# Vision block with routed experts: sums kept in the output tensor, and target rows for unused places of expert tiles

## The chip, the cores and the metric

The kernel runs on one core of a Trainium2 chip. The metric is the device time of one execution in microseconds (us); the median of three runs is compared.

## The reference

64 images of 196 tokens (12544 rows) of width 192. Patches are projected to tokens `h`; an attention branch with 12 heads is added; then a branch of 8 experts, of which each token takes the two with the highest router scores. Only this last part matters here:

```
score = relu(x @ Wr1.T + br1) @ Wr2.T + br2        # x = layernorm(h)
mask  = top 2 of 8;   w = softmax(where(mask, score, -inf))
for e in range(8):
    out += w[..., e:e+1] * (relu(x @ W1[e].T + b1[e]) @ W2[e].T + b2[e])
h = h + out
```

The result is an array of 12544 x 192 float32, which the kernel writes as `out_rows`.

## The kernel before

**Two phases.** The attention phase works through 32 pairs of images. For each pair SP stores `h` into the DRAM tensor `sums` (L405), loads it again (L410) and stores the attention sum there (L415); normalised rows go to `split_rows`. It ends at about 1170 us. Then `expert_phase` (L1318) runs.

**The expert phase.** All engines run the same loop over iterations `it`, each of six steps c = 0 to 5. Iterations 0 to 48 route one group of 256 tokens each: PE transposes and scores it, VectorE finds the two experts and their weights (`route`, `gates`), counts the place of each token within its expert (`find_place`), and GpSimd sends each row twice into `slots`, one list of rows for each expert (`send`, L1936). From iteration 10 on (`COMPUTE`) an expert tile of 512 rows is computed in each iteration: tile i = it - 10, 56 tiles (`NT`). `hidden` (L1558) makes the middle layer in six pieces; ScalarE writes the high part `mh` (L1885), VectorE the low part `ml` (L1797), and two steps later `project` (L1578) adds the piece to `y_bank`. In step 1 of the next iteration both engines evict with the gate (`y_out`, L1827 and L1893), and the first `project` of the next tile waits for that. GpSimd then issues four indirect DMAs of 128 rows each that add `y_out` to rows of `sums` (L1951); tile i waits until all adds of tile i-1 have landed (`added`).

**Which tiles.** Tiles 0 to 41 (`FULL`) are taken from the longest waiting list while routing goes on (`select`). The other 14 (`REST`) are planned at once, in the six steps of iteration 50 (`plan_rest`, L1717 to L1792, an increment of `plan` for each of 31 operations). A tile of these may overlap an earlier tile of its expert, may reach past the end of a list shorter than 512, or may be free (no rows left). Rows that don't count are sent to one of 512 extra rows behind the tokens in `sums`: `dest` is the token where `valid`, else the number of an extra row (`instead`, from `dummy_no`).

**Order around the change.** SP loads tile i two iterations ahead (`load_tile`, L1474): weights `wst`, transposed rows `xT`, and `tail` (token numbers and gates); for i >= 42 it waits for the whole plan (L1479), and each `tail` waits for the adds of tile i-3. On VectorE the order within a step is written out: `ml` of the piece, then the step's own work (gates, eviction, `find_place`, `select`, `tile_gates`, `route`), then the plan's part. `tile_gates` of tile i waits before `dest` until the adds of tile i-2 have landed. At the end SP waits for all adds and copies `sums` to the output:

```
sp.wait_ge(added, 16 * TJ * NT)
sp.dma_start(out.rearrange("(a b) e -> a (b e)", b=16),
             total_rows[0:ROWS_ALL].rearrange("(a b) e -> a (b e)", b=16)).then_inc(copied, 16)
sp.wait_ge(copied, 16)
```

## Time and profile before

| | us |
|---|---|
| median of 3 runs | 2125.47 (2125.39 to 2127.91) |
| the profiled execution, its own time | 2127.24 |
| its span, first to last instruction | 2125.5 |
| busy: PE / VectorE / ScalarE / GpSimd | 1868.0 / 1442.9 / 1280.5 / 1138.5 |
| mean granted TensorE clock | 0.934 |
| moved by DMA | 382.72 MB, mean 180 GB/s |

Engines in the rows: PE is TensorE, DVE VectorE, ACT ScalarE, POOL GpSimd, SPq the queue of SyncE. Times are us from the start of the span unless marked ns. A row names the line of the kernel, the operation, output<-input by the program's names without buffer numbers, and how often (x). In brackets or behind a bar stands how long the engine sat idle before it, and what ended that; such releasers are inferred, and where several things were awaited, the last by the profile is named. Ends of matmuls are modelled, so starts are compared, not ends.

### The profile page before, as it was taken

What the parts mean: (1) busy time and instruction counts of PE and PEld (TensorE: products, weight loads), DVE (VectorE), ACT (ScalarE), POOL (GpSimd) and SP (SyncE); (2) the same over time, 40 slices, a digit from 0 to 9 for tenths busy, and PEclk for the clock granted to TensorE, in tenths of its full rate; (3) what the DMA queues carried; (4) which work ended last, traced back from release to release, by engine and by line L of the source; (5) the groups of instructions that cost most, each with busy time, mean ns of one, the idle gap of its engine ahead of it and who ended that gap; (6) DMA issues with size and microseconds to landing.
All of it is one profiled execution on the core that took longest, in us unless ns stands there. A gap on an engine that the chain in (4) does not pass through costs nothing. (4 is left out here: it accounts for less than half of the span.)

```text
span 2125.5 us, 54282 instructions
## 1 busy us (share of the span) xinstructions
PE 1868.0 (88%) x17949; PEld 1387.1 (65%) x17949; DVE 1442.9 (68%) x4460; ACT 1280.5 (60%) x2661; POOL 1138.5 (54%) x1069
## 2 busy tenths in 40 slices
PE   4978988998888999889895679999999999999990
PEld 3656766666666766666663457777777777767760
DVE  4768888888988889888884446555555655554430
ACT  4758888888888888888886234434444343433330
POOL 4335564645555465555532346666666666654442
PEclk8879999999999999999986569999999999999995
DMA  4575665665656565565642267888787878799877
GB/s 152 169 204 168 192 207 160 196 181 173 194 176 198 175 194 170 180 187 188 192 146 87 84 171 185 203 189 210 180 208 189 197 204 187 199 195 180 189 146 196
DMA packets 362727, 382.72 MB, mean 180 GB/s; under 512 B 144532, under 2 KB 326096, under 8 KB 358288
## 3 DMA queue, kind: packets, MB, share of 16 engines
q1 hardware_dynamic: 320912, 338.66, 55.1%
q0 software_dynamic: 41664, 42.12, 11.5%
q8 instruction: 86, 1.41, 0.3%
q14 instruction: 65, 0.53, 0.1%
HBM read 232.83 MB, written 135.46 MB: 173 GB/s over the span
## 5 line engine op out<-in xcount | busy, mean ns | idle before, releaser
L1885 ACT ACTIVATE mh<-mid_bank 128x512 bf16<-128x512 f32 x336 | 201.0, 598 | 467.8 <-PE mid_bank L1576 356.6
L1797 DVE SCALAR_TENSOR_TENSOR ml<-mid_bank,mh 128x512 bf16<-128x512 f32 x336 | 231.8, 690 | 347.6 <-ACT mh L1885 338.6
L859 DVE TENSOR_REDUCE row_max<-s_bank 98x2 f32<-98x392 f32 x768 | 394.7, 556 | 57.6 <-PE s_bank L635 55.4
L1056 ACT ACTIVATE probs<-t_bank 98x392 f32<-98x392 f32 x768 | 340.5, 500 | 110.7 <-PE t_bank L651 106.6
L1951 POOL DMA_INDIRECT sums<-y_out,tail x168 | 265.2, 1579 | 171.5 <-DVE y_out L1827 124.1
L1590 PE MATMUL y_bank<-wst,mh 128*128 128x192 bf16 x1344 | 330.0, 246 | 8.7 <-DVE y_out L1827 8.4
L1593 PE MATMUL y_bank<-wst,ml 128*128 128x192 bf16 x1344 | 330.1, 246 | 0.0
L1592 PE MATMUL y_bank<-wst,mh 128*128 128x192 bf16 x1344 | 329.8, 245 | 0.0
L635 PE MATMUL s_bank<-k_stack,q_stack 96*98 96x196 f16 x1536 | 235.7, 261 | 56.9 <-DVE row_max L859 43.2
L1232 POOL TENSOR_TENSOR x_lo<-x_buf,x_hi 128x588 f16<-128x588 f32 x128 | 170.7, 1346 | 178.6 <-DVE x_b L924 76.2
L651 PE MATMUL t_bank<-q_stack,k_stack 104*98 104x196 f16 x1536 | 227.5, 261 | 38.2 <-ACT probs L1056 34.8
L1936 POOL DMA_INDIRECT slots<-row_r,spot x196 | 191.2, 976 | 97.4 <-issue 56.7
L635 PEld LDWEIGHTS s_bank<-k_stack,q_stack 96*98 96x98 f16 x1536 | 145.9, 127 | 107.3 <-DVE row_max L859 93.2
L651 PEld LDWEIGHTS t_bank<-q_stack,k_stack 104*98 104x98 f16 x1536 | 153.3, 129 | 80.0 <-ACT probs L1056 75.1
L543 PE MATMUL p_bank<-wtok_h,x_hi 128*98 128x192 f16 x768 | 193.6, 252 | 10.3 <-POOL x_lo L1232 10.2
L545 PE MATMUL p_bank<-wtok_h,x_lo 128*98 128x192 f16 x768 | 192.9, 251 | 0.0
L544 PE MATMUL p_bank<-wtok_l,x_hi 128*98 128x192 f16 x768 | 192.8, 251 | 0.0
L664 PE MATMUL o_bank<-probs,v_buf 98*32 98x196 f32 x3072 | 175.7, 348 | 4.4 <-ACT probs L1056 2.6
L1590 PEld LDWEIGHTS y_bank<-wst,mh 128*128 128x128 bf16 x1344 | 134.3, 100 | 41.9 <-issue 21.3
L1080 ACT COPY q_stack<-m_bank 8x784 f16<-8x784 f16 x192 | 154.6, 805 | 6.1 <-PE m_bank L675 1.5
L1592 PEld LDWEIGHTS y_bank<-wst,mh 128*128 128x128 bf16 x1344 | 131.0, 97 | 19.6
L1951 POOL DMA_INDIRECT sums<-y_out,dest x56 | 86.9, 1552 | 96.1 <-DMA sums<-y_out,dest 44.9
(236 smaller groups left out, 4530.7 us busy)
## 6 DMA issues: line engine op xcount, KB each, us to landing
wst<-packed SPq DMA_DIRECT2D x56, 1584.0 KB
x_buf<-in_x_t SPq DMA_DIRECT2D x32, 1176.0 KB, 7.9
q_stack<-stack_parts SPq DMA_DIRECT2D x288, 98.0 KB, 2.5
k_stack<-stack_parts SPq DMA_DIRECT2D x288, 98.0 KB, 2.6
stack_parts<-qk_hi SPq DMA_DIRECT2D x32, 588.0 KB, 2.9
stack_parts<-qk_lo SPq DMA_DIRECT2D x32, 588.0 KB, 3.1
sums<-h_buf SPq DMA_DIRECT2D x32, 294.0 KB
h_in<-sums SPq DMA_DIRECT2D x32, 294.0 KB
```

Of the source, the lines that this page charges most:

```text
L543: nc.tensor.matmul(out, x_hi[:, f, tokens], wtok_h[:, f, :], start=(f == 0), stop=False)
L545: ins = nc.tensor.matmul(out, x_lo[:, f, tokens], wtok_h[:, f, :], start=False, stop=(f == PCH - 1))
L635: last = nc.tensor.matmul(s_bank[hh % 2][0:HALF, u, 0:TOKENS], q_stack[st.q][0:PARTS, head, head_cols(st, u)], k_stack[st.q][0:PARTS, head ...
L651: last = nc.tensor.matmul(out, k_stack[st.q][:, head, head_cols(st, v)], q_stack[st.q][:, head, head_cols(st)], start=True, stop=True)
L859: nc.vector.reduce_max(row_max[st.odd][:, :, hh:hh + 1], s_bank[hh % 2][0:HALF, :, 0:TOKENS], AX.X).then_inc(max_ready, 1)
L1056: nc.scalar.activation(probs[st.odd][:, hh], t_bank[hh % 2][0:HALF, :, 0:TOKENS], ACT.Exp).then_inc(probs_ready, 1)
L1590: nc.tensor.matmul(o, mh[n % MID][:, cols], high, start=(c == 0 and j % 2 == 0), stop=False, skip_group_check=True)
L1592: nc.tensor.matmul(o, mh[n % MID][:, cols], low, start=False, stop=False, skip_group_check=True)
L1593: last = nc.tensor.matmul(o, ml[n % MID][:, cols], high, start=False, stop=False, skip_group_check=True)
L1797: nc.vector.scalar_tensor_tensor(ml[n % MID][:], mid_bank[n % MID_PS][:], 0.0, mh[n % MID][:], ALU.max, ALU.subtract).then_inc(ml_ready, 1)
L1885: nc.scalar.activation(mh[n % MID][:], mid_bank[n % MID_PS][:], ACT.Relu).then_inc(mh_ready, 1)
L1951: nc.gpsimd.indirect_dma_start(out=total_rows, out_offset=bass.IndirectOffsetOnAxis(ap=to, axis=0), in_=y_out[q][:, j, :], in_offset=None, ...
```

## The change

`sums` goes: the attention phase's rows and all adds go to the output tensor, and the copy at the end is gone. As the output has no extra rows, each row of a tile needs a real token, and one that occurs once in its DMA. Rows that only overlap keep their own token (`keep` now from `below`), rows of a free tile take tokens 0 to 511, and rows past the end of a short list take a token that the expert lacks. Their gate is multiplied by `valid`, so they add zeros. The tokens that an expert lacks are found among the first 1024 (`number_others` in iterations 1 to 4 numbers them, `place_others` in iteration 20 splits the numbers, `mark_others` on VectorE and `list_others` on PE in iterations 50 and 51 turn them into a list by a matmul with one-hot matrices, and `plan_spare_rows` in iteration 51 picks from it). `load_tile` waits for step 25 of the plan instead of the last. Constants: `SPARE_TILES` = 8, `HOT` = 3 buffers, `LIST_AT` = 20, `PLAN` = 39, `TILES_KNOWN` = 25.

```diff
 COMPUTE = SELECT + 2
 REST = NT - FULL
 AHEAD = 4
+SPARE_GROUPS = 2 * T // GT
+SPARE_TILES = SPARE_GROUPS * GTILES
+HOT = 3
 GATE_BLOCKS = 3
 
...
                 if i < FULL:
                     sp.wait_ge(selected, PICK * (i + 1))
                 else:
-                    sp.wait_ge(plan, PLAN)
+                    sp.wait_ge(plan, TILES_KNOWN)
...
             sp.wait_ge(added, 16 * TJ * NT)
-            sp.dma_start(out.rearrange("(a b) e -> a (b e)", b=16),
-                         total_rows[0:ROWS_ALL].rearrange("(a b) e -> a (b e)", b=16)).then_inc(copied, 16)
-            sp.wait_ge(copied, 16)
...
+
+            def list_others(e):
+                if 0 <= e < EXPERTS:
+                    pe.wait_ge(placed, PLACE * FGROUPS)
+                    pe.wait_ge(hot_ready, e + 1)
+                    for b in range(SPARE_TILES):
+                        last = nc.tensor.matmul(spare_ps[:, e, :], hot[e % HOT][:, b, :], listed[:, b, e, :],
+                                                start=(b == 0), stop=(b == SPARE_TILES - 1))
+                    last.then_inc(spares_ready, 1)
...
+                    list_others(FCH * (it - FULL - SELECT) + c - LAG)
                     if 0 <= n - LAG < FCH * NT:
                         project(n - LAG)
...
+            def number_others(g):
+                if 0 <= g < SPARE_GROUPS:
+                    shape = [P, GTILES, EXPERTS]
+                    if g == 0:
+                        dve.wait_ge(masks_set, 4)
+                    else:
+                        dve.wait_ge(number_ready, 3 * g)
+                    dve.wait_ge(placed, PLACE * g + 1)
+                    nc.vector.tensor_tensor(rank[:], place[:], first_slot[:].unsqueeze(1).to_broadcast(shape),
...
+                    nc.vector.scalar_tensor_tensor(away[:], chosen[g % 2][:], 2.0 * ROWS_ALL, rank[:], ALU.mult,
...
+                    nc.vector.scalar_tensor_tensor(number[:, GTILES * g:GTILES * (g + 1), :], away[:], float(GT * g),
+                                                   row_no[:, 0:GTILES].unsqueeze(2).to_broadcast(shape), ALU.add, ALU.add
...
+            def place_others(part):
+                shape = [P, SPARE_TILES, EXPERTS, TJ]
+                if part == 0:
+                    dve.wait_ge(number_ready, 3 * SPARE_GROUPS)
+                    nc.vector.tensor_copy(number_i[:], number[:]).then_inc(listed_ready, 1)
+                    dve.wait_ge(listed_ready, 1)
+                    nc.vector.tensor_scalar(column_i[:], number_i[:], 7, None, ALU.arith_shift_right
+                                            ).then_inc(listed_ready, 1)
+                    dve.wait_ge(listed_ready, 2)
+                    nc.vector.tensor_copy(column[:], column_i[:]).then_inc(listed_ready, 1)
+                elif part == 1:
+                    dve.wait_ge(listed_ready, 3)
+                    nc.vector.scalar_tensor_tensor(lane[:], column[:], -float(P), number[:], ALU.mult, ALU.add
+                                                   ).then_inc(listed_ready, 1)
+                    nc.vector.tensor_tensor(in_column[:], column[:].unsqueeze(3).to_broadcast(shape),
+                                            tile_no[:, 0:TJ].unsqueeze(1).unsqueeze(1).to_broadcast(shape),
+                                            ALU.is_equal).then_inc(listed_ready, 1)
+                elif part == 2:
+                    dve.wait_ge(listed_ready, LISTED - 1)
+                    nc.vector.tensor_tensor(listed[:], in_column[:],
+                                            token_f[:].unsqueeze(2).unsqueeze(2).to_broadcast(shape), ALU.mult
+                                            ).then_inc(listed_ready, 1)
+
+            def mark_others(e):
+                if 0 <= e < EXPERTS:
+                    shape = [P, SPARE_TILES, P]
+                    dve.wait_ge(listed_ready, LISTED)
+                    wait(dve, spares_ready, e - HOT + 1)
+                    nc.vector.tensor_tensor(hot[e % HOT][:], lane_no[:].unsqueeze(1).to_broadcast(shape),
+                                            lane[:, :, e:e + 1].to_broadcast(shape), ALU.is_equal
+                                            ).then_inc(hot_ready, 1)
+
...
-                    step(nc.vector.tensor_tensor(valid[:], above[:], below[:], ALU.mult))
...
                 elif part == 5:
+                    step(nc.vector.tensor_tensor(valid[:], above[:], below[:], ALU.mult))
+                    step(nc.vector.tensor_scalar(keep[:], below[:], -1.0, None, ALU.mult))
+                    step(nc.vector.tensor_scalar(unused[:], below[:], -1.0, 1.0, ALU.mult, ALU.add))
+                    step(nc.vector.tensor_scalar(is_free[:], rest_f[:], float(EXPERTS), None, ALU.is_ge))
+                    dve.wait_ge(plan, 33)
+
+            def plan_spare_rows(part):
+                def step(ins):
+                    ins.then_inc(plan, 1)
+
+                if part == 2:
+                    dve.wait_ge(spares_ready, EXPERTS)
+                    step(nc.vector.tensor_copy(other_row[:], spare_ps))
+                    dve.wait_ge(plan, 34)
+                elif part == 3:
+                    shape = [P, REST, TJ, EXPERTS]
+                    step(nc.vector.tensor_tensor(past_other[:], is_expert[:].unsqueeze(2).to_broadcast(shape),
+                                                 other_row[:].rearrange("p e j -> p j e").unsqueeze(1)
+                                                 .to_broadcast(shape), ALU.mult))
+                    dve.wait_ge(plan, 35)
+                    step(nc.vector.reduce_sum(other_f[:].unsqueeze(3), past_other[:], AX.X))
+                elif part == 4:
                     shape = [P, REST, TJ]
-                    nc.vector.tensor_scalar(keep[:], valid[:], -1.0, None, ALU.mult)
-                    step(nc.vector.tensor_scalar(unused[:], valid[:], -1.0, 1.0, ALU.mult, ALU.add))
-                    dve.wait_ge(plan, 30)
-                    step(nc.vector.tensor_tensor(instead[:], unused[:], dummy_no[:].unsqueeze(1).to_broadcast(shape),
-                                                 ALU.mult))
+                    step(nc.vector.tensor_tensor(spread[:], row_no[:].unsqueeze(1).to_broadcast(shape),
+                                                 is_free[:].unsqueeze(2).to_broadcast(shape), ALU.mult))
+                    dve.wait_ge(plan, 37)
+                    step(nc.vector.tensor_tensor(harmless[:], spread[:], other_f[:], ALU.add))
+                    dve.wait_ge(plan, 38)
+                    step(nc.vector.tensor_tensor(instead[:], unused[:], harmless[:], ALU.mult))
...
@@ -1814,9 +1921,13 @@
                     wait(dve, added, 16 * TJ * (i - 1))
                     nc.vector.tensor_tensor(dest[q][:], kept[:], instead[:, i - FULL, :], ALU.bitwise_or
                                             ).then_inc(gate_step, 1)
+                    nc.vector.tensor_tensor(gate_sum[:], gate_m[:], words[:, :, 3], ALU.add).then_inc(gate_step, 1)
+                    dve.wait_ge(gate_step, base + 4)
+                    nc.vector.tensor_tensor(gate[q][:], gate_sum[:], valid[:, i - FULL, :], ALU.mult
+                                            ).then_inc(gate_step, 1)
                 else:
                     dve.wait_ge(gate_step, base + 1)
-                nc.vector.tensor_tensor(gate[q][:], gate_m[:], words[:, :, 3], ALU.add).then_inc(gate_step, 1)
+                    nc.vector.tensor_tensor(gate[q][:], gate_m[:], words[:, :, 3], ALU.add).then_inc(gate_step, 1)
...
                     elif c == 3:
+                        number_others(it - 1)
                         select(it - SELECT)
...
                         route(it)
                     if it == FULL + SELECT:
                         plan_rest(c)
+                    elif it == FULL + SELECT + 1:
+                        plan_spare_rows(c)
+                    elif it == LIST_AT:
+                        place_others(c)
+                    mark_others(FCH * (it - FULL - SELECT) + c)
...
-            nc.gpsimd.iota(dummy_no[:], [[P, TJ]], base=ROWS_ALL, channel_multiplier=1,
+            nc.gpsimd.iota(lane_no[:], [[1, P]], base=0, channel_multiplier=0,
                            allow_small_or_imprecise_dtypes=True).then_inc(masks_set, 1)
+            nc.gpsimd.iota(token_f[:].rearrange("p (g j) -> p g j", g=SPARE_GROUPS), [[GT, SPARE_GROUPS], [1, GTILES]],
+                           base=0, channel_multiplier=GTILES, allow_small_or_imprecise_dtypes=True
+                           ).then_inc(masks_set, 1)
...
-    sums = nc.dram_tensor("sums", (ROWS_ALL + T, DIM), F32).ap()
...
-                        stack_parts, by_pair(sums[0:ROWS_ALL]), by_pair(split), router)
-        expert_phase(nc, packed, slots, sums, split.rearrange("(g t) e -> g t e", t=GT), router, out)
+                        stack_parts, by_pair(out), by_pair(split), router)
+        expert_phase(nc, packed, slots, out, split.rearrange("(g t) e -> g t e", t=GT), router)
```

## Rows read from the trace of the kernel before

**Rows 1.** Windows: from:to and length, busy us per engine (xcount), PEclk, DMA share, GB/s.

```profile
2092.00:2126.00 34.00, 0.00 (x0) 0.00 (x0) 0.00 (x0) 0.00 (x0) 0.00 (x0) 0.50 0.89 283
```

**Rows 2.** DMA issues: xcount, KB each, median us to landing.

```profile
out_rows<-sums SPq DMA_DIRECT2D x1, 9408.0 KB, 32.8
```

**Rows 3.** Timeline of GpSimd and of SP: start us, length, instruction, idle before it.

```profile
2035.02 1.55 POOL L1951 DMA_INDIRECT sums<-y_out,dest  x1 [6.81 <-DVE gate L1819]
...
2040.59 1.55 POOL L1951 DMA_INDIRECT sums<-y_out,dest  x1 [0.30 <-issue]
2049.01 1.55 POOL L1951 DMA_INDIRECT sums<-y_out,dest  x1 [6.87 <-DVE gate L1819]
...
2088.73 1.55 POOL L1951 DMA_INDIRECT sums<-y_out,dest  x1 [0.30 <-issue]
...
2092.26 0.65 SPq L1507 DMA_DIRECT2D out_rows<-sums  x1
```

**Rows 4.** Chain that ended last, in order of time: start us, us, what.

```profile
2040.59 7.65 DMA sums<-y_out,dest
...
2079.03 3.35 DMA sums<-y_out,dest
```

**Rows 5.** Timeline of VectorE.

```profile
1873.07 0.74 DVE L1827 TENSOR_SCALAR y_out<-y_bank,gate 128x192 f32<-128x192 f32 x2 [1.41 <-DMA sums<-y_out,tail]
...
1885.85 0.74 DVE L1827 TENSOR_SCALAR y_out<-y_bank,gate 128x192 f32<-128x192 f32 x2
...
2048.33 0.16 DVE L1815 TENSOR_TENSOR dest<-kept,instead 128x4 int32<-128x4 int32 x1 [2.43 <-DMA sums<-y_out,dest]
```

**Rows 6.** Timeline of GpSimd, first adds of tiles 36 and 37.

```profile
1829.62 1.61 POOL L1951 DMA_INDIRECT sums<-y_out,tail  x1 [3.01 <-DVE y_out L1827]
...
1845.11 1.61 POOL L1951 DMA_INDIRECT sums<-y_out,tail  x1 [2.97 <-DVE y_out L1827]
```

**Rows 7.** Timeline of VectorE, early iteration, scores of a group.

```profile
1190.72 0.17 DVE L1636 TENSOR_TENSOR score<-small_bank,br_rows 128x16 f32<-128x16 f32 x1 [3.87 <-PE small_bank L1542]
```

**Rows 8.** Groups by line and shape, VectorE: busy us, mean ns | idle before.

```profile
L943 DVE TENSOR_TENSOR tilde<-beside,padded 128x1176 f32<-128x1176 f32 x32 | 43.8, 1368 | 0.0
...
L1742 DVE TENSOR_TENSOR past<-tile_no,scan 128x112 f32<-128x112 f32 x1 | 0.3, 266 | 0.0
```

**Rows 9.** The same groups in the stretch 1870 to 1885.8 alone.

```profile
L1797 DVE SCALAR_TENSOR_TENSOR ml<-mid_bank,mh 128x512 bf16<-128x512 f32 x7 | 4.8, 692 | 3.4 <-ACT mh L1885 2.5 <-DVE expert_i L1772 0.6 <-DVE done_f L1762 0.2
L1827 DVE TENSOR_SCALAR y_out<-y_bank,gate 128x192 f32<-128x192 f32 x2 | 0.7, 414 | 1.4 <-DMA sums<-y_out,tail 1.4
```

**Rows 10.** Timeline of PE, first projection of tile 41.

```profile
1886.73 0.24 PE L1590 MATMUL y_bank<-wst,mh 128*128 128x192 bf16 x1
```

**Rows 11.** Timeline of GpSimd, first adds of tiles 40 and 41.

```profile
1886.86 1.55 POOL L1951 DMA_INDIRECT sums<-y_out,tail  x1 [5.25 <-DVE y_out L1827]
...
1900.10 1.55 POOL L1951 DMA_INDIRECT sums<-y_out,tail  x1 [6.12 <-DVE y_out L1827]
```

**Rows 12.** Timeline of PE: matmuls of 8 and of 192 columns.

```profile
1841.00 0.17 PE L1551 MATMUL small_bank<-chosen,before 128*128 128x8 bf16 x1
...
1841.10 0.17 PE L1555 MATMUL small_bank<-chosen,ones 128*128 128x8 bf16 x1
...
2029.91 0.25 PE L1592 MATMUL y_bank<-wst,mh 128*128 128x192 bf16 x1
2029.99 0.25 PE L1593 MATMUL y_bank<-wst,ml 128*128 128x192 bf16 x1
```

**Rows 13.** Waits of SP, 1860 to 1900: waiter <- what, us, times, longest.

```profile
SPq L1480 <- DVE instead L1791: 4.6, 1, 4.6
```

**Rows 14.** Windows, columns as in rows 1.

```profile
1962.00:2062.00 100.00, 98.34 (x816) 70.04 (x813) 40.70 (x92) 36.97 (x69) 44.29 (x29) 1.00 0.91 182
```

**Rows 15.** Groups by line and shape, GpSimd from 1200 us on.

```profile
L1951 POOL DMA_INDIRECT sums<-y_out,tail x168 | 265.2, 1579 | 171.5 <-DVE y_out L1827 124.1 <-issue 38.4 <-DMA sums<-y_out,tail 9.0
...
L1951 POOL DMA_INDIRECT sums<-y_out,dest x56 | 86.9, 1552 | 96.1 <-DMA sums<-y_out,dest 44.9 <-DVE gate L1819 27.0 <-issue 16.2
```

46 lines of the change are left out of this document (38 added, 8 removed).

## The prediction

> **What bounds the kernel now.** I read the page's slices first, then the busy time by stretch, then the end of the timeline, and from there backwards along the chain of waits. The reader is to see three stretches.
>
> (a) The last 34 us belong to one transfer. After 2092 no engine is busy while the DMA engines work at 0.89 [rows 1]: that is the copy of L1507, issued at 2092.26 and landed 32.8 us later, at 2125.06 [rows 2, 3]. It starts 0.15 us after the last adding DMA lands: that was issued at 2088.73 [rows 3], and with 3.35 us to land, as the one of 2079.03 had [rows 4], it lands at 2092.1. Nothing overlaps the copy and only 0.4 us follow it.
>
> (b) In tiles 42 to 55 the expert phase runs to the adding DMAs, not to PE. GpSimd issues four per tile, and tile i waits until those of tile i-1 have landed. One link: first issue at 2035.02, last at 2040.59 (5.6 us), 7.65 us to land, 0.77 us until the next tile's first issue at 2049.01: 14.0 us [rows 3, 4]. (The gate named as releaser there is the next tile's; GpSimd does not wait for it.) VectorE even stands 2.43 us before `dest`, waiting for such a landing [rows 5]. A tile of PE work takes about 12.8 us there, which is the distance from one tile's eviction at 1873.07 to the next at 1885.85 [rows 5].
>
> (c) Before, up to tile 39, the distance from one tile's adds to the next is 15.5 us and they start when `y_out` is ready [rows 6]: PE and the router set the pace, and the chain of adds, 14.0 us as above, has some 1.5 us of slack.
>
> **The change part by part.**
>
> The copy goes. What is then last is the landing of the last adds at 2092.1 and the same 0.4 us behind it. Gain: 2125.06 - 2092.1 = 33.0 us, all on the path, since nothing lay beside it [rows 1 to 4]. The stores and loads of the attention phase, and all adds, now go to the output tensor instead of `sums`: same shapes, same queues, same counts. No row shows 768-byte adds to the output. The nearest row is the copy itself, which writes 9408 KB into it in 32.8 us, 294 GB/s [rows 2], so the output takes writes at a good rate; I put the difference at nothing, with 2 us either way over 56 tiles and 96 row transfers for other addresses.
>
> Numbering the tokens (`number_others`, 3 small VectorE operations in each of four early iterations). An operation of 16 elements starts about 0.2 us after its predecessor when it waits for it, so 0.6 us. VectorE stands idle 3.87 us in each of these iterations until the next scores come [rows 7]: hidden. Without that cover it would be 2.4 us. The GpSimd constants (one iota more, one larger) lie ahead of its wait for VectorE's memsets: hidden too.
>
> Listing (`place_others`, 6 operations at iteration 20, of 64 to 256 elements). By the size law below about 1.8 us over three steps. VectorE has 1 us and more of idle time in most steps, but `ml` and the eviction behind it are needed by PE: 0.2 us, between 0 and 1.8.
>
> Marking (`mark_others`, 8 operations on VectorE at iterations 50 and 51). This is the term that costs. Size: 128x1024 with two float32 inputs. The 128x1176 operation of L943 takes 1368 ns and the 128x112 one of L1742 266 ns [rows 8], so 1.036 ns an element, 1.21 us for 1024, and 1.13 us from start to start, as successors start 0.08 us before an end. Place: each is issued at the end of a step, behind `plan_rest`, and ahead of the next step's `ml`, so seven of them stand ahead of the eviction of tile 40. That stretch (1869.4 to 1885.85) has VectorE idle 3.4 us before `ml` and 1.4 us before `y_out` [rows 9]. Of these 4.8 us some 0.3 us before `y_out` and 0.2 us of waiting for its own result remain, so 4.3 us can be filled. Added: 7 x 1.13 + 0.1 (one more small plan operation) = 8.0 us. Overflow: 3.7 us. Who waits: PE, whose first projection of tile 41 came at 1886.73, directly after `y_out` of 1885.85 was written [rows 5, 10]. So PE, the eviction of tile 41 and the adds of tiles 40 and 41 move by 3.7 us. Both starts of adds were released by `y_out` [rows 11], and from 42 on each follows from the landing before it, so the shift stays to the end. What could take part of it back: the weights of tiles 43 and 44 were loaded beside these adds, and with the adds later the loads are ahead of them. Bounds 0.5 and 5.
>
> Counting on PE (`list_others`, 64 matmuls of 128x128 weights on 4 columns). Nearest rows: the five matmuls of 8 columns of `count` start 25 ns apart [rows 12], so 8 x 25 ns = 0.2 us for each expert, 1.6 us in all. Those of seven experts fall before the projection that waits for the eviction anyway, the eighth after it: 0.2 us. Upper bound: each of them priced as a 192-column matmul of L1592 and L1593, 80 ns apart [rows 12], 5.1 us in all, of which 0.6 us falls after that wait. The Trainium skill speaks against the short spacing ("TensorE: Matmul & The Clock Gate", section "Back-to-back issue gap"): in a stream where each matmul has its own weight load it gives about 81 ns for each at 128 columns and says that the isolated figure counts too little at small sizes. The trace disagrees for the small form; by the page the term would be 0.65 us instead of 0.2.
>
> The plan. SP loaded tile 42 only after the whole plan, waiting 4.6 us for `instead` [rows 13]; now it waits for step 25, which comes earlier by two parts but behind four marks: about 1.5 us sooner. PE never waited for that load: nothing. `plan_spare_rows` waits on VectorE for PE's eighth group; behind it stands one `ml`, and PE needs that two steps later: nothing (0 to 1 us). The two extra small operations of `tile_gates` in the last 14 tiles stand behind the wait for the adds; PE has 14.0 - 12.8 = 1.2 us of slack there against some 0.15 us: nothing.
>
> Rows that add zeros now hit real tokens instead of 512 rows behind them. Each add still moves the same 128 rows: nothing.
>
> Sum: -33.0 + 3.7 + 0.2 + 0.2 = -28.9 us. The profiled execution took 2127.24 us with a span of 2125.5, so it would take 2098.3, with a span of 2096.6. The median of the runs shown is 1.77 us lower, so I predict 2125.47 - 28.9 = 2096.6 us.
>
> **The rivals.**
>
> The shift is taken back (15%). For it: the DMA engines are at 0.91 in the tiles after 45 [rows 14], so the chain of adds partly waits for bandwidth, and loads that ran ahead leave it free. Against: loads are themselves released by landings. If 3 us of the 3.7 vanish: 2093.6.
>
> The marking costs more (14%). For it: four adds of tile 39 and of tile 40 are issued in just that stretch. Only the most general row bears on it: GpSimd's add instruction takes 1579 ns beside router work on VectorE and 1552 ns in the last tiles without it [rows 15], so VectorE disturbs it little. If each of 8 issues is held for half a mark, 0.6 us, 5 us come on top: 2101.6. The Trainium skill ("SBUF — State Buffer", on the shared port pair) says that a VectorE operation with two SBUF inputs and a GpSimd one exclude each other for a whole instruction; by its rule the issues would be blocked, and this is the case it argues for. The trace shows 27 ns.
>
> Adds into the output land later (4%, slower). Mechanism: adds read and write 768-byte rows of a tensor that so far only took one large copy. Place: the last leg of each tile's chain. Price: x us per landing costs 14x in tiles 42 to 55, and beyond the slack of 1.5 us also 42(x - 1.5) before them [rows 6]. It eats the gain of 28.9 us where 56x = 28.9 + 63, x = 1.64 us (a landing of 9.3 us for 7.65). At x = 2.1 us it costs 29.4 + 25.2 = 54.6 us: 2151. Against: nothing in the copy's row hints at a slow tensor.
>
> The copy's end was not the program's end (1%): if some fixed work of like length follows the last transfer, no change, 2125. Against: 0.4 us follow it in the trace.
>
> **How the numbers follow.** Forecast 63%, 2094.5 to 2098.8. Taken back 15% (2092.5 to 2094.5). Costs more 14% (2098.8 to 2105). Other addresses gain more than 33 us 3%. Slower 4%, none 1%. The range 2091 to 2102 leaves out the last three, 8%, and the upper half of the costlier case, 7%; the few per cent that remain are for the small terms put at nothing. A difference of 0.2% (4.3 us) is what a measurement of this kernel can tell from none. Faster: 63 + 15 + 14 + 3 = 95%; same 1%; slower 4%.
>
> **What would show it.** No transfer after the last add, and the span's end within 1 us of that landing. At 1870 to 1890 eight 128x1024 operations of about 1.2 us on VectorE, the eviction of tile 40 about 3.7 us later against that of tile 39, and PE idle before the first projection of tile 41. Starts of adds 42 to 52 still 13 to 14 us apart. Iterations 1 to 4 and 20 as long as before. The prediction is wrong if the landing of the adds has changed, if the 15.5 us pace of tiles up to 39 has changed, or if the marks are hidden.

## The result and the profile after

| kernel | median of the device time | range, runs |
|---|---|---|
| before | 2125.49 us | 2125.39 to 2127.91, 4 |
| after | 2102.77 us | 2097.00 to 2105.89, 4 |

Ratio 0.9888, interval 0.9871 to 0.9906: the change gives 22.7 us, where 28.9 was predicted. The median lies 0.8 us above the upper end of the predicted range, 2091 to 2102 us. The profiled execution of after took 2097.0 us, with a span of 2095.2 us; it is the fastest of the four.

The end first. These are GpSimd's timeline (start us, length, instruction, idle before it) and windows (columns as in rows 1) of after, behind the last step of work.

```profile
2081.46 1.55 POOL L2071 DMA_INDIRECT out_rows<-y_out,dest  x1 [2.82 <-DMA out_rows<-y_out,dest]
...
2087.03 1.55 POOL L2071 DMA_INDIRECT out_rows<-y_out,dest  x1 [0.30 <-issue]
```

```profile
2089.00:2090.00 1.00, 0.00 (x0) 0.00 (x0) 0.00 (x0) 0.00 (x0) 0.00 (x0) 0.50 0.90 95
2090.00:2091.00 1.00, 0.00 (x0) 0.00 (x0) 0.00 (x0) 0.00 (x0) 0.00 (x0) 0.50 0.04 4
2091.00:2093.00 2.00, 0.00 (x0) 0.00 (x0) 0.00 (x0) 0.00 (x0) 0.00 (x0) 0.50 0.00 0
2093.00:2095.20 2.20, 0.00 (x0) 0.00 (x0) 0.00 (x0) 0.00 (x0) 0.00 (x0) 0.50 0.00 0
```

No transfer follows the last add, as the change says. But the transfers stop at 2090.3 and the span ends at 2095.2. From the last issue to the end are 8.2 us. By the chain of waits the adds before it take 3.5 to 3.6 us to land:

```profile
2052.90 7.26 DMA out_rows<-y_out,dest
...
2066.51 3.49 DMA out_rows<-y_out,dest
...
2077.09 3.59 DMA out_rows<-y_out,dest
```

So the last add lands at about 2090.6 (an estimate: 2087.03 and 3.5 to 3.6), and 4.6 us of the span lie behind it, in which no engine computes and nothing is transferred. The prediction had 0.4 us there.

Then the marking. VectorE's timeline of after, around the evictions of tiles 39 and 40:

```profile
1872.93 0.73 DVE L1938 TENSOR_SCALAR y_out<-y_bank,gate 128x192 f32<-128x192 f32 x2
...
1874.85 1.23 DVE L1773 TENSOR_TENSOR hot<-lane_no,lane 128x1024 f16<-128x1024 f32 x1
1875.99 0.68 DVE L1904 SCALAR_TENSOR_TENSOR ml<-mid_bank,mh 128x512 bf16<-128x512 f32 x1
...
1877.78 1.22 DVE L1773 TENSOR_TENSOR hot<-lane_no,lane 128x1024 f16<-128x1024 f32 x1
...
1880.45 1.22 DVE L1773 TENSOR_TENSOR hot<-lane_no,lane 128x1024 f16<-128x1024 f32 x1
...
1888.92 0.73 DVE L1938 TENSOR_SCALAR y_out<-y_bank,gate 128x192 f32<-128x192 f32 x2
1889.58 1.22 DVE L1773 TENSOR_TENSOR hot<-lane_no,lane 128x1024 f16<-128x1024 f32 x1
...
1892.26 0.19 DVE L1883 COPY other_row<-small_bank 128x32 f32<-128x32 f32 x1 [0.87 <-PE small_bank L1588]
...
1901.89 0.74 DVE L1938 TENSOR_SCALAR y_out<-y_bank,gate 128x192 f32<-128x192 f32 x2
```

A mark takes 1.23 us and the next instruction starts 1.14 us after it. The two `y_out` of tiles 39 and 40 are 16.0 us apart, for 12.8 in [rows 5]: 3.2 us more. The next distance, 13.0 us, is 0.2 longer than 12.8. VectorE has no idle time left ahead of any of these `y_out`. Four marks are waited for by PE; this is one of eight groups of `list_others` on PE's timeline:

```profile
1876.22 0.34 PE L1588 MATMUL small_bank<-listed,hot 128*128 128x4 f16 x8 [0.18 <-DVE hot L1773]
```

Eight matmuls of 4 columns in 0.34 us with the last one's 0.16 us in it, so seven distances in 0.18 us: 25 ns apart.

GpSimd's timeline of after, adds of tiles 38 to 42:

```profile
1860.21 1.61 POOL L2071 DMA_INDIRECT out_rows<-y_out,tail  x1 [2.67 <-DVE y_out L1938]
...
1874.60 1.70 POOL L2071 DMA_INDIRECT out_rows<-y_out,tail  x1 [1.36 <-DMA out_rows<-y_out,tail]
1876.61 1.57 POOL L2071 DMA_INDIRECT out_rows<-y_out,tail  x1 [0.30 <-issue]
1878.48 1.96 POOL L2071 DMA_INDIRECT out_rows<-y_out,tail  x1 [0.30 <-issue]
1880.75 2.35 POOL L2071 DMA_INDIRECT out_rows<-y_out,tail  x1 [0.30 <-issue]
1889.93 2.28 POOL L2071 DMA_INDIRECT out_rows<-y_out,tail  x1 [6.84 <-DVE y_out L1938]
1892.52 1.55 POOL L2071 DMA_INDIRECT out_rows<-y_out,tail  x1 [0.30 <-issue]
...
1904.00 1.55 POOL L2071 DMA_INDIRECT out_rows<-y_out,tail  x1 [6.20 <-DMA out_rows<-y_out,tail]
...
1917.00 1.55 POOL L2071 DMA_INDIRECT out_rows<-y_out,dest  x1 [5.88 <-DMA out_rows<-y_out,tail]
```

Tile 38 starts its adds within 0.3 us of before (1860.21 for 1859.96), so the attention phase, the routing and the tiles up to 38 took the same time in these two executions. Tile 40 starts 3.1 us later than in [rows 11], tile 41 3.9 us later. Tile 42 starts only 1.8 us later (1917.00 for 1915.21), tile 53 2.0 us earlier, and the last issue of all comes at 2087.03, 1.7 us earlier than 2088.73 [rows 3]. So against this execution of before something gave back more than the whole shift, 2.1 us of it between tiles 41 and 42 and 3.8 us between tiles 42 and 53, and the end of the program cost more than expected. The experiments had to tell whether either is the kernel's or the execution's.

One measure is used for all of them, from GpSimd's timeline: the distance from the first add of tile 42 to the first add of tile 53 ("the chain"; before 147.8 us, after 143.9), and from the last issue to the end of the span ("the end"; before 36.8, after 8.2).

### The profile page after: what moved, and what is told of

Same layout as the page of the kernel before. It is cut to its first block and busy times, and to the rows that moved or that the text cites. A ratio compares the mean times of both kernels' runs of the same rounds, so it can differ in the third digit from the quotient of the medians.

```text
span 2095.2 us, 54476 instructions
## 1 busy us (share of the span) xinstructions
PE 1865.1 (89%) x18013; PEld 1385.8 (66%) x18013; DVE 1457.7 (70%) x4506; ACT 1278.6 (61%) x2661; POOL 1140.0 (54%) x1070
## 5 line engine op out<-in xcount | busy, mean ns | idle before, releaser
L2071 POOL DMA_INDIRECT out_rows<-y_out,tail x168 | 267.1, 1590 | 176.6 <-DVE y_out L1938 111.6
L1624 PEld LDWEIGHTS y_bank<-wst,mh 128*128 128x128 bf16 x1344 | 134.2, 100 | 43.3 <-issue 22.1
L2071 POOL DMA_INDIRECT out_rows<-y_out,dest x56 | 86.9, 1552 | 90.5 <-DMA out_rows<-y_out,dest 68.4
```

The source lines that it names most:

```text
L1624: nc.tensor.matmul(o, mh[n % MID][:, cols], high, start=(c == 0 and j % 2 == 0), stop=False, skip_group_check=True)
L2071: nc.gpsimd.indirect_dma_start(out=total_rows, out_offset=bass.IndirectOffsetOnAxis(ap=to, axis=0), in_=y_out[q][:, j, :], in_offset=None, ...
```

## The experiments

Each kernel was timed beside the kernel before on its own chip, and three chips were used after the first. The table gives the times; "gain" is the median of before less that of the kernel, on the same chip. Evictions are the distance from tile 39's to tile 40's, in the profiled execution. The profiled execution is one of the runs and need not be a typical one: e1's is the slowest of its five (2088.75 us), e5's the fastest of its six (2090.56 us) and e6's the second slowest of its six (2103.93 us).

| kernel | chip | median, us (range, runs) | ratio (interval) | gain | evictions | chain | end |
|---|---|---|---|---|---|---|---|
| e1 no copy | 2 | 2081.48 (2077.9 to 2088.8, 5) | 0.9839 (0.9825 to 0.9852) | 32.7 | 12.8 | 149.7 | 8.2 |
| e2 listing, sums, no copy | 2 | 2087.02 (2083.0 to 2088.2, 4) | 0.9865 (0.9850 to 0.9881) | 27.1 | 16.2 | 146.0 | 8.2 |
| e3 after, again | 2 | 2086.60 (2084.0 to 2086.9, 4) | 0.9863 (0.9848 to 0.9878) | 27.6 | 16.0 | 146.2 | 8.3 |
| e4 marks early | 2 | 2084.54 (2077.3 to 2090.5, 5) | 0.9856 (0.9834 to 0.9878) | 29.6 | 13.8 | 144.8 | 8.3 |
| e5 no copy, again | 3 | 2095.77 (2090.6 to 2097.0, 6) | 0.9871 (0.9848 to 0.9895) | 25.5 | 12.8 | 143.8 | 8.3 |
| e6 marks alone | 3 | 2099.05 (2094.2 to 2106.0, 6) | 0.9887 (0.9860 to 0.9914) | 22.3 | 16.2 | 146.4 | 8.2 |
| e7 old targets | 3 | 2096.67 (2094.7 to 2099.0, 6) | 0.9874 (0.9851 to 0.9898) | 24.6 | 16.4 | 142.4 | 8.2 |
| e8 other SBUF places | 3 | 2096.59 (2091.2 to 2099.9, 6) | 0.9874 (0.9847 to 0.9900) | 24.7 | 12.9 | 143.4 | 8.2 |
| e9 listing in the fill | 4 | 2101.23 (2095.1 to 2103.1, 5) | 0.9883 (0.9864 to 0.9903) | 22.1 | 12.8 | 145.4 | 8.3 |
| e10 after, third time | 4 | 2100.66 (2096.9 to 2103.7, 5) | 0.9889 (0.9872 to 0.9906) | 22.7 | 16.3 | 143.1 | 8.2 |
| e11 no copy, third time | 4 | 2096.82 (2088.9 to 2097.6, 5) | 0.9860 (0.9840 to 0.9879) | 26.5 | 12.8 | 143.4 | 8.2 |
| e12 light loads | 4 | 2088.59 (2081.1 to 2095.2, 6) | 0.9831 (0.9808 to 0.9854) | 34.7 | 12.8 | 138.5 | 8.2 |

The kernel before had 2114.16 (2111.05 to 2118.66, 9 runs), 2121.31 (2117.80 to 2131.51, 11) and 2123.31 us (2120.14 to 2128.12, 11) on chips 2, 3 and 4.

### e1: the copy alone goes

```diff
-            sp.dma_start(out.rearrange("(a b) e -> a (b e)", b=16),
-                         total_rows[0:ROWS_ALL].rearrange("(a b) e -> a (b e)", b=16)).then_inc(copied, 16)
+            sp.dma_start(out.rearrange("(a b) e -> a (b e)", b=16)[0:1],
+                         total_rows[0:ROWS_ALL].rearrange("(a b) e -> a (b e)", b=16)[0:1]).then_inc(copied, 16)
```

> The kernel before, where the copy at the end moves only the first 16 rows (the other rows of the output are left unwritten). Open after the result: the changed kernel's median is 2102.8 us where the sum gave 2096.6, and its runs lie between 2097.0 and 2105.9 where those of before lie within 2.5 us. Theory A (the copy was worth 33 us, and what is missing lies in the change's new work or in the output tensor): 2125.5 - 33.0 + 2 for the small transfer = 2094 us, with runs within 3 us of each other. Rival B (the end of the chain of adds varies by itself from run to run, and the copy's wait hid nothing of it): runs spread by 5 us or more here too, median 2094 to 2100.

Measured: 32.7 us gained, with runs 10.9 us apart, as the rival expected; those of before are 7.6 us apart on this chip, so the wider spread can't be laid to the missing copy. The timeline of e1 ends so:

```profile
2078.69 1.55 POOL L1951 DMA_INDIRECT sums<-y_out,dest  x1 [0.30 <-issue]
2082.21 0.65 SPq L1507 DMA_DIRECT2D out_rows<-sums  x1
```

Its span is 2086.9 us. The small copy lands 2.2 us after its issue, at 2084.4, and still the span ends only 8.2 us behind the last add's issue, exactly as in after, where no copy follows. So the end follows the adds' landing (about 2082.2, 4.7 us before the end), not the small copy's. SP's own waits at the end say who is late. In e1 (waiter, what, us, times, longest):

```profile
SPq L1321 <- PEq L1321: 2.2, 1, 2.2
SPq L1321 <- DMA out_rows<-sums: 1.6, 1, 1.6
```

In after:

```profile
SPq L1324 <- PEq L1324: 4.5, 1, 4.5
```

And in the kernel before:

```profile
SPq L1321 <- DMA out_rows<-sums: 32.1, 1, 32.1
SPq L1321 <- PEq L1321: 0.2, 1, 0.2
```

Where no transfer keeps SP, it stands 4.5 us for a signal that the profile puts down to PE's sequencer; beside a copy of 2.2 us, 2.2 us are left of that; beside the copy of 32.8 us, 0.2. That fits an end of the program that was always there, with the copy lying over it. Going by these traces, taking the copy away gains 36.8 - 8.2 = 28.6 us, not 33.0.

### e2 and e3: is it the output tensor?

e3 is the kernel after, unchanged. e2 is after with `sums` kept as the place of all adds and the same copy of 16 rows as in e1:

```diff
+            sp.dma_start(out.rearrange("(a b) e -> a (b e)", b=16)[0:1],
+                         total_rows[0:ROWS_ALL].rearrange("(a b) e -> a (b e)", b=16)[0:1]).then_inc(copied, 16)
+            sp.wait_ge(copied, 16)
...
-                        stack_parts, by_pair(out), by_pair(split), router)
+                        stack_parts, by_pair(sums[0:ROWS_ALL]), by_pair(split), router)
```

> The changed kernel with all its listing, but with the separate tensor for the sums as before, and a copy of 16 rows only at the end (the rest of the output is left unwritten). Theory A1 (the missing 6 us come from adding into the output tensor): this is 6 us faster than the changed kernel, about 2097 + 2 for the small transfer. Theory A2 (they come from the listing, marking on VectorE and what it moves in the chain of adds): this is as slow as the changed kernel, about 2103 + 2 = 2105, and 8 to 11 us slower than the run without copy and without listing. The shift of one marking stretch of 3.7 us alone would give 4 us between those two.

> The changed kernel again, unchanged, for its spread and for a second trace. Expected: median 2101 to 2104, runs between 2096 and 2107. Its trace shows where a run that is slower than 2097 lost its time: in the adds of tiles 42 to 55 (theory: starts of adds more than 13.3 us apart on average) or before iteration 50 (rival: the adds of tile 38 start later than 1861).

Measured: 2087.02 and 2086.60 us, with chains of 146.0 and 146.2 us and the same end. Adding into the output costs what adding into `sums` costs, within the spread of the runs. e2 and e3 are 5.5 and 5.1 us slower than e1, where theory A2 had 8 to 11 for e2: by the medians that is what the listing and marking cost here. e3's time was expected at 2101 to 2104 us, as on the first chip; before, too, is 11 us faster on this chip. The gain of after itself is 27.6 us on it and was 22.7 on the first, for the same program.

### e4: one mark per tile, in earlier iterations

The marks lie at 1446 to 1552 us, one in each iteration, and have eight buffers instead of three.

```diff
-HOT = 3
+HOT = 8
...
-                    mark_others(FCH * (it - FULL - SELECT) + c)
+                    if c == 4:
+                        mark_others(it - LIST_AT - 2)
```

> The changed kernel with the eight marking operations moved from iterations 50 and 51 to iterations 22 to 29, one in each, in step 4, into eight buffers instead of three; the rest is the same. My step (seven marks of 1.13 us overflow VectorE's idle time by 3.7 us and PE waits for it): the eviction of tile 40 comes 3 us earlier than in the changed kernel, and the median is 3 to 4 us lower, about 2099. Rival (the shift is taken back in tiles 42 to 48, as the first trace after the change suggests, and the spread comes from the chain of adds): the eviction moves but the median stays within 1.5 us of the changed kernel.

Measured: 2084.54 us, 2.1 us below e3 with intervals that overlap. VectorE's timeline of e4 has the evictions of tiles 39 and 40 here:

```profile
1859.29 0.73 DVE L1938 TENSOR_SCALAR y_out<-y_bank,gate 128x192 f32<-128x192 f32 x2
...
1873.07 0.74 DVE L1938 TENSOR_SCALAR y_out<-y_bank,gate 128x192 f32<-128x192 f32 x2 [0.20 <-DMA out_rows<-y_out,tail]
```

They are 13.8 us apart: 1.0 us more than 12.8 instead of 3.2, and VectorE has idle time ahead of the second again. What is left lies beside PE's matmuls of the counting, which stayed where they were, eight groups of 8 x 25 ns, some 1.6 us; e9 below, which moves them too, has 12.8. So 2.2 us are gone from this place, where 3 were expected. That the time too is 2.1 us lower does not show that they reach the end: its spread covers zero, and in the traces the adds of tile 42 start 156.6 us after those of tile 38 in e4 and 156.7 us in e3, so nothing of the 2.2 us is left there. e4 is still 3.1 us above e1.

### e5 to e8: what gave the shift back in the chain?

After's chain was 3.9 us shorter than before's, and e1's was the longest of all. Four theories were open: it belongs to the marks, to the addresses of the unused rows, to the place of the buffers in SBUF, or to the execution.

e5 is e1 once more, on another chip.

> The kernel before with a copy of only 16 rows at the end (the rest of the output is left unwritten), once more, as the base for the three kernels beside it. Expected: 32 to 33 us under the kernel before on this chip. Its adds of tiles 42 to 53 take 12 links of the chain; both traces so far gave 147.8 and 149.7 us from the start of tile 42 to that of tile 53, and landings of 7.3 to 8.1 us for tiles 49 to 52: the same again if this belongs to the kernel and not to the execution.

e6 is e1 plus the eight marks, whose result nobody reads:

```diff
+            def mark_others(e):
+                if 0 <= e < EXPERTS:
+                    shape = [P, 8, P]
+                    dve.wait_ge(lane_set, 2)
+                    wait(dve, hot_ready, e - 2)
+                    nc.vector.tensor_tensor(hot[e % 3][:], lane_no[:].unsqueeze(1).to_broadcast(shape),
+                                            lane[:, :, e:e + 1].to_broadcast(shape), ALU.is_equal
+                                            ).then_inc(hot_ready, 1)
...
                         plan_rest(c)
+                    mark_others(FCH * (it - FULL - SELECT) + c)
```

> The kernel of e5 with one addition: eight VectorE operations of 128x1024 at the places of the marking (iterations 50 and 51), whose result nobody reads. My step: seven overflow VectorE's idle time, the eviction of tile 40 comes 3.0 to 3.7 us later. Theory S (the shift stays to the end, as predicted): this kernel is 3 to 4 us slower than e5. Theory R (it is taken back, since landings depend on how far the adds lag behind PE and a later PE gets a shorter chain): the stretch from tile 42 to 53 is 3 us shorter than in e5, about 144 to 146 us, and the medians are within 1.5 us.

e7 is e2 with the old targets of unused rows, the 512 rows behind the tokens (`keep` and `unused` are made from `valid` again, too):

```diff
-                    step(nc.vector.tensor_tensor(instead[:], unused[:], harmless[:], ALU.mult))
+                    step(nc.vector.tensor_tensor(instead[:], unused[:], dummy_no[:].unsqueeze(1).to_broadcast(shape), ALU.mult))
```

> The changed kernel with all its listing and marking and the separate tensor for the sums, with a copy of 16 rows only (the rest of the output is left unwritten), but rows that don't count go to the 512 extra rows as before the change. Theory D (the targets decide the landings: the same few extra rows are slower than real tokens): tiles 42 to 53 take 148 to 150 us as in e5. Theory R: they take 144 to 147 us as in the other kernels with marking, whatever the targets.

e8 is e1 with two tensors that nobody uses, which push all later ones to the places that they have in after:

```diff
+        hot = sb("hot", [P, 3, 1024], F16)
+        number_pad = sb("number_pad", [P, 1534])
```

> The kernel of e5 with two unused tensors of 12280 bytes per partition in front of the weights' buffers in SBUF, so that all later buffers of the expert phase lie where the changed kernel has them; nothing else differs, and nothing is computed with them. Theory L (the place of the buffers in SBUF decides the landings): tiles 42 to 53 take 144 to 147 us and the median is 3 us under e5. Theories R and D: no difference to e5, within 1 us.

Measured, on one chip: e5 2095.77, e6 2099.05, e7 2096.67, e8 2096.59 us. The evictions of tiles 39 and 40 in e6:

```profile
1876.16 0.73 DVE L1841 TENSOR_SCALAR y_out<-y_bank,gate 128x192 f32<-128x192 f32 x2
...
1892.33 0.73 DVE L1841 TENSOR_SCALAR y_out<-y_bank,gate 128x192 f32<-128x192 f32 x2
```

16.2 us apart: the marks alone make the whole stretch of 3.2 to 3.6 us; counting, placing and targets add nothing that shows. The median of e6 is 3.3 us above that of e5, but their runs overlap (2094.2 to 2106.0 and 2090.6 to 2097.0 us), and the times alone don't show that the shift reaches the end. VectorE's evictions show how far it goes. Those of tiles 39 and 55, the last one, in e11 (e1's kernel once more, below):

```profile
1876.22 0.74 DVE L1827 TENSOR_SCALAR y_out<-y_bank,gate 128x192 f32<-128x192 f32 x2 [1.31 <-DMA sums<-y_out,tail]
...
2078.46 0.74 DVE L1827 TENSOR_SCALAR y_out<-y_bank,gate 128x192 f32<-128x192 f32 x2 [1.98 <-DMA sums<-y_out,dest]
```

That of tile 55 in e6, and in before:

```profile
2081.78 0.74 DVE L1841 TENSOR_SCALAR y_out<-y_bank,gate 128x192 f32<-128x192 f32 x2 [1.98 <-DMA sums<-y_out,dest]
```

```profile
2077.39 0.74 DVE L1827 TENSOR_SCALAR y_out<-y_bank,gate 128x192 f32<-128x192 f32 x2 [1.98 <-PE y_bank L1597]
```

From tile 39 to tile 55 it is 202.2 us in e5 and e11 (203.0 in e8), and 205.6 to 206.0 us in all six profiles with the marks at this place (after, e2, e3, e6, e7, e10). Between tiles 41 and 54 their evictions follow each other at 12.8 us. So the whole shift, 3.4 to 3.8 us, reaches the last eviction. In before it is 204.3 us and in e1 205.4, since there the evictions of tiles 53 and 54 were held: they come 14.0 and 13.7 us (before), 14.5 and 14.3 us (e1) after the one ahead, and VectorE had stood 2.4 to 2.9 us before `dest`, waiting for adds. The row of 2.43 us in [rows 5] is one of the two such places of before.

What scatters lies behind the evictions. The last add is issued 8.1 to 8.5 us after the last eviction in after, e5, e7, e8 and e11, and 9.3 to 12.2 us after it in the others, before with 11.3 among them (e12, below, has 6.6). Both kinds occur with marks and without. Against before's trace after's has 3.4 us more by the marks, 2.1 less in held evictions and 2.9 less behind the last one: that is the shift "taken back".

What gave it back in the first trace falls to no edit. e5 is the very program of e1, and its chain took 143.8 us where e1's took 149.7. So a difference of 6 us in the chain comes between two executions of the same program on two chips, and before's 147.8 against after's 143.9 needs no cause in the change. The theory that targets decide (e7: 142.4) and the one that the places decide (e8: 143.4, like e5) fell with it: neither edit moved the chain away from 143.8 by more than that scatter, and e7's 142.4 lies outside what either theory had said for it. The expectation of theory R in e6, a chain shorter than e5's, failed as well: it is 2.6 us longer. e5 itself had been expected 32 to 33 us under before and came out at 25.5.

### e9, e10 and e11: the listing where VectorE and PE have room

e9 moves all of it, marks and counting, into iterations 6 to 9, ahead of the first expert tile; e10 is after once more and e11 is e1 once more. The core of e9's edit:

```diff
-        LIST_AT = 2 * COMPUTE
+        LIST_AT = SPARE_GROUPS + 1
...
-                    list_others(FCH * (it - FULL - SELECT) + c - LAG)
+                    if c == 5 and it > LIST_AT:
+                        list_others(2 * (it - LIST_AT - 1))
+                        list_others(2 * (it - LIST_AT - 1) + 1)
...
-                    mark_others(FCH * (it - FULL - SELECT) + c)
+                    if c in (3, 4) and it > LIST_AT:
+                        mark_others(2 * (it - LIST_AT - 1) + c - 3)
```

> The changed kernel with the whole listing moved into the expert phase's first iterations, before any tile is computed: splitting in iteration 5, two marks each in iterations 6 to 9 where VectorE waits 3.9 us for the scores, the matmuls behind each pair, in another PSUM bank, and the result read in iteration 9. Theory M (the marking at iteration 50 costs what the trace shows, 3.1 to 3.4 us at the eviction of tile 40, and most of it reaches the end): median 3 to 4 us under e10 (the changed kernel beside it) and equal to e11 (no copy, no listing) within 1.5 us; the gap between the evictions of tiles 39 and 40 is 12.8 us again; first adds of tile 0 not later than in e10 by more than 0.5 us. Rival R (the shift is taken back in tiles 42 to 53): the gap is 12.8 us too, but the median lies within 1.5 us of e10.

> The changed kernel, as the base of e9 and e11. Expected 27 to 29 us under the kernel before on this chip; the eviction of tile 40 comes 16.0 us after that of tile 39. The stretch from the adds of tile 42 to those of tile 53 is anything from 142 to 150 us, since it was 143.8 and 149.7 us in two executions of one kernel.

> The kernel before with a copy of only 16 rows at the end (the rest of the output is left unwritten), third time. Expected: 3 to 4 us under e10 if the marking's shift reaches the end (theory M), within 1.5 us if it is taken back (rival R). On two chips it was 5.1 us under the changed kernel and 3.3 us under the one with the marks alone.

Measured: e9 2101.23, e10 2100.66, e11 2096.82 us. In e9's timeline of VectorE the stretch is gone:

```profile
1877.05 0.74 DVE L1939 TENSOR_SCALAR y_out<-y_bank,gate 128x192 f32<-128x192 f32 x2 [1.47 <-DMA out_rows<-y_out,tail]
...
1889.83 0.74 DVE L1939 TENSOR_SCALAR y_out<-y_bank,gate 128x192 f32<-128x192 f32 x2
```

12.8 us, as before the change. The time did not follow: e9 is 0.6 us above e10 and 4.4 above e11, where theory M had 3 to 4 us under the one and the same as the other. So this experiment failed to give a better kernel, and the median came out as rival R said. The listing is not free in its new place: the adds of tile 0 start at 1276.27 us for 1273.74 in e10, 2.5 us later, where at most 0.5 was expected. Of the 3.5 us that the evictions gain on e10's (12.8 for 16.3), 1.0 us is paid ahead of tile 38, whose adds start at 1863.88 for 1862.90, and 2.3 us in the chain (145.4 for 143.1), which is inside that chain's scatter; the last issue comes at 2091.23 for 2090.68. Two evictions of e9 were held (those of tiles 50 and 52, 13.5 and 13.0 us after the one ahead), and its last add is issued 11.0 us after the last eviction, for 9.3 in e10 and 8.4 in e11. Whether the loss in the chain is the kernel's or the execution's stays open: the runs of e9 spread over 8 us. e10 had been expected 27 to 29 us under before and gave 22.7; e11 lies 3.8 us under e10, as theory M said. No version was found that clearly beats the kernel after.

### e12: is it the weight loads that make the landings long?

e12 is e1 with the weight loads of the last 11 tiles cut to 384 columns, 192 KB for 1584 KB by the list of DMA issues (so the full load has 3168 columns, not the 3552 of the expectation); those tiles compute with stale weights.

```diff
-                sp.dma_start(wst[q][:], packed.rearrange("(e t) p n -> e t p n", t=2)[bass.ds(e, 1)]
-                             .rearrange("o t p n -> p (o t) n")).then_inc(w_in[q], 16)
+                some = PACK if i < FULL + DEEP else PART
+                sp.dma_start(wst[q][:, :, 0:some], packed.rearrange("(e t) p n -> e t p n", t=2)[bass.ds(e, 1)]
+                             .rearrange("o t p n -> p (o t) n")[:, :, 0:some]).then_inc(w_in[q], 16)
```

> The kernel of e11 where the weights of tiles 45 to 55 are loaded only in part (384 of 3552 columns, the rest of the buffer keeps old weights, so these tiles' results are not the reference's; and a copy of only 16 rows). Theory C (the landings of 6 to 8 us in tiles 42 to 53 are waits behind the weight loads, and their sum varies from execution to execution): landings fall to about 3.5 us as in tiles 54 and 55, adds start when y_out is ready, the stretch from 42 to 53 is 141 us (11 times 12.8), tile 55's adds come 3 to 6 us earlier, the median is 2 to 6 us under e11 and the spread is smaller. Rival P (the scattered rows themselves take 6 us or more): landings stay above 5.5 us and the median moves by less than 1 us.

Measured: 2088.59 us, 8.2 us below e11 on the same chip, with intervals that overlap and a spread that is wider (14.1 us for 8.7), not smaller as expected, and a chain of 138.5 us for 143.4. Windows and GpSimd's timeline of e11:

```profile
1962.00:2062.00 100.00, 100.00 (x832) 71.60 (x831) 41.87 (x95) 37.41 (x70) 46.55 (x31) 1.00 0.88 189
```

```profile
1982.87 1.55 POOL L1951 DMA_INDIRECT sums<-y_out,dest  x1 [5.67 <-DMA sums<-y_out,dest]
...
1995.78 1.55 POOL L1951 DMA_INDIRECT sums<-y_out,dest  x1 [5.78 <-DMA sums<-y_out,dest]
```

The same of e12:

```profile
1962.00:2062.00 100.00, 100.00 (x833) 71.54 (x831) 42.20 (x95) 37.80 (x72) 49.68 (x32) 1.00 0.55 75
```

```profile
1989.36 1.55 POOL L1952 DMA_INDIRECT sums<-y_out,dest  x1 [5.66 <-DVE y_out L1828]
...
2002.13 1.55 POOL L1952 DMA_INDIRECT sums<-y_out,dest  x1 [5.66 <-DVE y_out L1828]
```

With 75 instead of 189 GB/s moved, the adds are released by `y_out` and no longer by the landing before them, and they come 12.8 us apart, which is PE's pace. So the adds of tiles 42 to 52 wait for landings only because these share the DMA engines with the weight loads. They don't hold PE in e11: PE is busy throughout the stretch in both, and from the eviction of tile 39 to that of tile 55 both take 202.2 us. What the light loads gain in the trace is the lag behind the last eviction, 6.6 us for 8.4. That is 1.8 of the 8.2 us; in these two traces 2.9 us more lie ahead of the eviction of tile 39, where the kernels are the same, and the rest is between executions.

## Why the prediction was right, and where it was off

**The copy goes, and the adds become the end: right.** No transfer follows the last add, and the whole gain comes from there.

**What the time owes to luck.** 2102.8 us lies in the band that the prediction gave to the rival "the marking costs more", 2098.8 to 2105. That mechanism is not what put it there: it is worth 2.1 us at most (below), and the larger miss is the end of the program.

**"The same 0.4 us behind it": wrong, and this is the term that was mis-sized.** The sum took 33.0 us for the copy. The row of 0.4 us behind the copy's landing was read as the length of the program's end. By e1 and after it was only what the copy had left uncovered of it. Measured, the span ends 8.2 or 8.3 us after the last issue in all thirteen profiles without the large copy (after and e1 to e12), 4.6 to 4.7 us after the landing, against 36.8 in before: 28.6 us, 4.4 less than in the sum. The prediction's own sign, an end within 1 us of the last landing, did not come. The medians can't tell 28.6 from 33.0: the four measurements without copy and without listing gained 32.7, 25.5, 24.7 and 26.5 us (e1, e5, e8, e11), 27.4 in the mean. The traces can, with 8.2 to 8.3 us in each. The rival "the copy's end was not the program's end" had the right mechanism; the prediction gave it 1% because it let it take the whole gain and didn't ask for a part.

**"In tiles 42 to 55 the expert phase runs to the adding DMAs, not to PE": wrong as it stands.** PE sets the pace of the evictions, 12.8 us for each tile, in before as well, but for the two held ones. The adds fall behind it: the link of 14.0 us and the wait of 2.43 us before `dest` were rows of the worst place, and the eleven links of before's chain are 13.4 us in the mean, after's 13.1 (12.5 to 14.5). No term of the sum was sized by it, and the shift stays for another reason than the one given: PE carries it to the last eviction, and the adds follow from there.

**The marks: right in place, kind and nearly in size.** Forecast were 1.21 us each and 1.13 from start to start, measured are 1.23 and 1.14. Of seven marks ahead of the eviction, 4.3 us of cover were to leave 3.7; the stretch came out at 3.2 us in after and 3.2 to 3.6 in e2, e3, e6, e7 and e10. VectorE has no idle time ahead of `y_out` in after, for which the sum had left 0.5 us, and that is the difference. e6 shows that the marks alone do it.

**The shift stays to the end: shown up to the last eviction, and borne out behind it as far as the scatter lets one see.** All six profiles with the marks in place have 3.4 to 3.8 us more between the evictions of tiles 39 and 55 than e5 and e11. By the times, against the kernel without copy on the same chip, the kernels with marks at the same place lose 5.5 and 5.1 us (e2, e3 over e1), 3.3 and 0.9 (e6, e7 over e5) and 3.8 (e10 over e11): 3.7 in the mean, for 4.1 predicted. e8, without any mark, differs by 0.8 from e5. A single pair can't size the shift. All five have its sign, but they share three measurements of the kernel without copy, and e4 and e9, which have no marks at this place, lose 3.1 and 4.4 us as well, so these differences are no proof of it. In the first pair of traces the shift seems to be taken back whole (the last issue 1.7 us earlier), which was the rival "taken back". e5 against e1 shows that a single trace can't settle this: executions of one program differ by 6 us in that chain.

**Counting on PE: right.** 25 ns apart, as in [rows 12], and 0.2 us for a group; the eighth one adds 0.2 us to the eviction of tile 41. The 81 ns that the Trainium skill gives ("TensorE: Matmul & The Clock Gate", section "Back-to-back issue gap") are for 128 columns and don't carry over to 4, though each of these matmuls has a weight load of its own; the issue floor of about 25 ns that the same section has for 1 to 64 columns, and which the prediction passed over, agrees. What the sum did not name: PE waits 0.18 to 0.50 us for a mark four times, 1.2 us in all, before the stretch that waits for the eviction anyway; so it cost nothing.

**The marking costs more: the mechanism exists, at a smaller price.** Add issues on GpSimd take 1.55 to 1.61 us in before [rows 6, 11]. In after, the one of 1889.93 starts 0.35 us into the mark of 1889.58 and takes 2.28; the one of 1880.75 starts 0.30 into a mark and takes 2.35; the one of 1878.48 starts 0.7 into one and takes 1.96; the one of 1874.60 starts ahead of a mark and takes 1.70. So an issue that meets a running mark grows by nearly what the mark has left: by 0.73 to 0.80 us with 0.87 to 0.92 left, by 0.41 with 0.52. The Trainium skill says of the shared port pair ("SBUF — State Buffer", section "SBUF: two separate sides") that a VectorE operation with two SBUF inputs and a GpSimd operation that reads SBUF lock each other out for a whole instruction: the trace agrees in kind. But only four of the eight issues grow by it, by 2.1 us together, and of those only 0.7 us lie where tile 40's adds are the next thing waited for. The 27 ns of [rows 15] was an average over issues of which few meet so long an operation, and was the wrong row for this question. Five us on top would have made some 9 us of e6 over e5, which came to 3.3.

**Place_others, number_others, the plan, the gates, the targets, the place of the sums at nothing: right within what can be told.** Tile 38 starts 0.3 us from where it did; e2 and e3 differ by 0.4 us; e7 is 2.4 us under e6, less than their runs spread. SP loads tile 42 at 1881.89, 1.7 us sooner than before, as forecast with 1.5, and PE had not waited for it.

**The sum again, with the measured terms:** -28.6 for the copy and +3.7 for the listing (the mean of the five pairs, and within the 3.4 to 3.8 of the evictions) are -24.9 us, 2100.6 us. The three measurements of the changed kernel gave 22.7, 27.6 and 22.7. The median of the first was 6.2 us above the forecast: 4.4 us of that are the end of the program, the other 1.8 are less than the gain of one kernel differs between chips.

**What stays open.** Why landings beside weight loads take 6 us in one execution and 8 in another, and with that how far the last adds lag behind the last eviction; why e9, whose eviction stretch is gone, has no shorter time; and what the last 4.6 us of the program are.

## What to carry to other kernels

What lies behind the last transfer in a trace need not be the length of the program's end; it may be only what that transfer left uncovered of it, as here. When a long tail transfer is to go, count the gain from the last instruction of the other engines to the end of a program that has no such tail, and where no such trace exists, allow for a part that the transfer covered (4.4 us here). Before a shift is said to be taken back further on, profile the unchanged kernel twice: the scatter of a chain that shares the DMA engines may be larger than the shift. Then follow the engine with the steady pace: here the evictions showed to 0.4 us what neither the times nor the chain of adds could. And of a large VectorE operation ask not only for its length but for what GpSimd issues while it runs.

## What the runs showed of the hardware

- 8.2 to 8.3 us lie between the issue of the last add and the end of the span in all thirteen profiles without the large copy, whether a short transfer follows or none; with landings of 3.5 to 3.6 us that leaves an estimated 4.6 to 4.7 us behind the landing. In after SP waits 4.5 us of them for a signal put down to PE's sequencer; what is done in them no row shows.
- A scattered add of 128 rows of 768 bytes lands in 3.4 to 3.6 us when it has the DMA engines to itself (tiles 53 and 54 of before, after and e1) and in 6 to 8 us beside the loads (1584 KB of weights for each tile). With those cut, the adds are again at PE's pace.
- The same program took 143.4, 143.8 and 149.7 us for the same 11 tiles in three executions on three chips (e11, e5, e1), with the granted clock at 1.00 in that stretch. The clock of the whole span does not explain the scatter from run to run: e4's slowest run (2090.5 us) had 0.939 and its fastest (2077.3 us) 0.947, but e6's slowest (2106.0 us) and fastest (2094.2 us) both had 0.944.
- Eight matmuls of 4 columns, each with 128x128 weights of its own, follow each other at 25 ns.
- Issues of adds on GpSimd that meet a running VectorE operation of 128x1024 with two SBUF inputs take 1.96 to 2.35 us where others take 1.55 to 1.61 (three in after); one that starts 0.25 us ahead of it takes 1.70.
